# Attention row sums: four diagonal rounds of each second half move from Pool's adds to TensorE's ones matmuls

## The chip, the cores and the metric

The program runs on one core of one Trainium2 chip. The metric is the device time of one execution in microseconds (us), lowest to highest over three runs, with the median as the figure that is compared. One more execution was taken by the hardware profiler; its trace gives all durations below.

## What is computed

The program is a chain of four blocks on an input of 2 x 1024 rows of 1024, each added to its input after a layer norm. The change is in the third, causal attention with 32 heads of 32 columns. Eight groups of four heads exist:

```python
def _L1_attn_ref(x, Wq, Wkv, Wo, bo):
    ...
    q = jnp.dot(x, Wq).reshape(b, t, H, HD).transpose(0, 2, 1, 3)
    kv = jnp.dot(x, Wkv).reshape(b, t, G, 2, HD).transpose(2, 3, 0, 1, 4)
    ...
    scores = jnp.einsum('bhqd,bhkd->bhqk', q, k)
    causal = jnp.triu(jnp.ones((t, t), dtype=bool), 1)
    scores = jnp.where(causal[None, None], -jnp.inf, scores)
    weights = jax.nn.softmax(scores * (1.0 / HD ** 0.5), axis=-1)
    ctx = jnp.einsum('bhqk,bhkd->bhqd', weights, v)
    ctx = ctx.transpose(0, 2, 1, 3).reshape(b, t, d)
    return jnp.dot(ctx, Wo) + bo
```

Here b is 2, t is 1024, H is 32, HD is 32. The softmax's denominator is the sum of the exponentials over the keys of a query; the change is about how that sum is formed.

## The kernel before

The classes StageA to StageD hold the four blocks, and each engine has a hand-written order of its instructions in each. Attention is StageC (lines 1542 to 2415). Its main loop has 16 **items** `o`, one for each batch half and head group, and each item has 48 **slots** `s`: 12 **rounds** `r` of four heads `g`. A round is a key tile `kt` of 128 keys against one **half** of the queries, 512 wide. The table ROUNDS (line 1493) lists them: rounds 0 to 3 are the first half (key tiles 0 to 3, all on the diagonal, 512, 384, 256 and 128 queries wide), rounds 4 to 7 are the second half's key tiles 0 to 3 (each 512 wide, below the diagonal), and rounds 8 to 11 its key tiles 4 to 7 (diagonal: 512, 384, 256 and 128 wide).

In one slot the engines do this:

- **TensorE** (`pe`, from line 2024) computes one score tile (`pe_score`, line 1978) into one of three PSUM banks, then one tile of the row-maximum pass for a slot 60 further on (`pe_amax`, line 1960), then on some slots three matmuls of the projection for a later item (`pe_job`, lines 1936 to 1938). At the second slot of each round (`g == 1`) it multiplies the exponentials of the round two before by the values (`pe_pv`, line 1993): four matmuls of 32 output rows each, in four column groups of the array. At slot 38 there is one small transpose of the maxima (line 1966).
- **ScalarE** (`act_exp`, line 2147) writes the exponentials of a round into one of three buffers P. It waits until the round three before has been multiplied (`pv_s`) and added up (`psum_s` or `pair_s`).
- **Pool** (`pool`, from line 2369) masks the diagonal block of a diagonal round (the affine select, line 2389), and adds the round's exponentials to a running sum S in SBUF, four heads at a time (lines 2383, 2385, 2406, 2407 and 2410). VectorE makes the sum of rounds 4 and 5 (`dve_pair`, line 2244). Pool also multiplies the finished contexts by the reciprocal sums (`pool_mul`, line 2367), and for two weights computes the low parts (`POOL_W`, line 2231).
- **TensorE** then sums S over its 128 partitions by matmuls with a matrix of ones (`pe_sum`, line 2019), four matmuls of 512 columns: the first half at slot 20, the second at slot 5 of the next item. ScalarE copies that bank out (`act_evac`) at the next slots 22 and 6.
- **VectorE** reduces each tile of the maximum pass (`dve_amax`, lines 2298 and 2302), and splits projections and weights into high and low parts.

Three PSUM banks (3, 4 and 6) serve the maximum pass, the transposes and the row sums in turn. The function `tables` hands them out at build time: `turn(o, a)` takes the bank that was given back longest ago, and `keeps` is the list of banks to be taken. A bank's next user waits for the engine that read the last one (`pe_turn`).

Four items, BY_ROUND (4, 5, 14 and 15), already sum their first half another way: `pe_sums` (line 2009) multiplies each round's exponentials by the ones matrix right behind the values' product, adding in one PSUM bank over the four rounds, and Pool adds nothing there. They hold a bank from slot 9 to slot 21. Of items 14 and 15, VectorE adds the later rounds (LAST, `dve_last`).

The semaphore counts that go with Pool's adds are computed by `adds(o, r)`.

SP's queue loads and stores; among its transfers are the rows of maxima (`sp_mrow`, tile c_mT to c_Q, issued at slot 40 for the next item), without which the next item's first score cannot start.

## Time and profile before the change

| | us |
|---|---|
| median of 3 runs | 2275.1 |
| lowest, highest run | 2274.99, 2286.18 |
| profiled execution, first to last instruction (span) | 2287.7 |
| TensorE matmuls busy | 2130.1 (93%) |
| TensorE weight loads busy | 1514.9 (66%) |
| VectorE busy | 1433.9 (63%) |
| Pool busy | 998.4 (44%) |
| ScalarE busy | 919.1 (40%) |

The profiler gives no time of its own execution apart from the span, so the span stands for it; it is 0.55% above the median of the runs. Busy time is the time an engine worked, whatever else ran beside it. A matmul's end in the trace is modelled, and the next may start before it: the distance from one start to the next is what a matmul takes of TensorE. "<-" behind an idle time names what ended it.

The granted clock of TensorE was 0.964 of full speed over the span. Attention's main loop runs from about 1014 us to 1790 us of the span.

### The profile page before, as it was taken

How to read it: one execution, taken by the hardware profiler on the slowest of the kernel's cores; microseconds unless marked ns; L12 is line 12 of the kernel's file. 1: busy time of each engine (PE TensorE's matmuls, PEld its weight loads, DVE VectorE, ACT ScalarE, POOL GpSimd, SP SyncE). 2: the span in 40 equal slices, each digit the busy share in tenths (PEclk: the TensorE clock that was granted, in tenths of full speed). 3: DMA queues.
4: the chain of work that ended last, by engine and by line, in shares of the span. 5: the costliest groups of instructions: out<-in, count | busy, mean ns of one | idle time of the engine just before them, and what ended most of it. 6: DMA issues, size and time to landing. Idle time of an engine off the chain costs nothing.

```text
span 2287.7 us, 30903 instructions
## 1 busy us (share of the span) xinstructions
PE 2130.1 (93%) x10720; PEld 1514.9 (66%) x10720; DVE 1433.9 (63%) x3291; ACT 919.1 (40%) x1675; POOL 998.4 (44%) x866
## 2 busy tenths in 40 slices
PE   5889997799999999989999999899998999999998
PEld 4755555688888878855555555555554687676677
DVE  8865688677777664287665667567668555443333
ACT  5644465333333323225554455455555332221111
POOL 1343476544444430016885577667873232120000
PEclk9899998999999999989999999999987999999999
DMA  5210147222222238531224722322223475343232
GB/s 185 83 81 1 59 148 254 112 74 74 74 74 74 74 108 288 138 75 50 70 63 100 203 65 75 77 69 72 57 67 117 155 255 166 111 172 123 100 122 92
DMA packets 139594, 249.25 MB, mean 109 GB/s; under 512 B 26910, under 2 KB 69790, under 8 KB 139216
## 3 DMA queue, kind: packets, MB, share of 16 engines
q1 hardware_dynamic: 128432, 227.37, 31.3%
q10 hardware_dynamic: 11008, 19.93, 2.8%
q8 instruction: 85, 1.39, 0.3%
q14 instruction: 69, 0.57, 0.1%
HBM read 139.48 MB, written 76.02 MB: 94 GB/s over the span
## 4 chain that ended last, share of the span: by engine, by line
PE 63%; POOL 12%; DVE 8%; DMA 3%; issue 3%; SPq 2%; ACT 2%; ACTq 1%; DVEq 0%; POOLq 0%
POOL c_S L2410 7%; PE PS L2579 5%; PE PS L2583 5%; PE PS L2580 5%; PE PS L2622 5%; PE PS L1119 3%; PE PS L1118 3%; PE PS L1120 3%; PE PS L1978 3%; PE PS L1960 2%; PE PS L1993 2%; PE PS L1151 2%; PE PS L1153 2%; PE PS L1152 2%; PE PS L1936 2%
## 5 line engine op out<-in xcount | busy, mean ns | idle before, releaser
L2147 ACT ACTIVATE c_P<-PS 128x512 f32<-128x512 f32 (+3 forms) x768 | 357.6, 494 | 331.8 <-PE PS L1978 311.4
L1960 PE MATMUL PS<-c_K,c_Q 96*128 96x512 f32 (+3 forms) x768 | 278.6, 373 | 19.8 <-DVE cst L2302 14.5
L1978 PE MATMUL PS<-c_Q,c_K 97*128 97x512 f32 (+3 forms) x768 | 284.3, 384 | 12.4 <-DMA c_Q<-c_mT 9.5
L2410 POOL TENSOR_TENSOR c_S<-c_S,c_P 128x2048 f32<-128x2048 f32 (+3 forms) x94 | 272.6, 2901 | 8.5
L1978 PEld LDWEIGHTS PS<-c_Q,c_K 97*128 97x128 f32 x768 | 148.3, 195 | 181.4 <-ACT c_P L2147 97.9
L2298 DVE TENSOR_REDUCE cst<-PS 128x1 f32<-128x512 f32 x256 | 175.9, 687 | 91.6 <-PE PS L1960 91.1
L1960 PEld LDWEIGHTS PS<-c_K,c_Q 96*128 96x128 f32 x768 | 151.4, 197 | 75.9 <-DVE cst L2302 38.6
L1993 PE MATMUL PS<-c_P,c_V 128*32 128x512 f32 (+3 forms) x1536 | 170.0, 515 | 15.1 <-ACT c_P L2147 8.2
L2302 DVE CUSTOM_DVE_ANT_0 PS<-PS,maskw,cst 128x128 f32<-128x128 f32 (+3 forms) x256 | 142.8, 558 | 58.1 <-PE PS L1960 42.2
L199 POOL TENSOR_TENSOR maskw<-maskw,mhalf 128x1 f32<-128x1 f32 x64 | 36.5, 570 | 323.1 <-DVE maskw L168 323.0
L2302 DVE CUSTOM_DVE_ANT_0 PS<-PS,maskw 128x128 f32<-128x128 f32 (+3 forms) x256 | 126.4, 504 | 73.7 <-PE PS L1960 71.5
L1363 DVE SCALAR_TENSOR_TENSOR b_pr<-b_g,b_a 128x460 f32<-128x460 f32 x192 | 159.9, 869 | 1.7
L1251 ACT ACTIVATE b_g<-PS 128x460 f32<-128x460 f32 x96 | 53.1, 553 | 263.7 <-PE PS L1125 263.7
L2389 POOL TENSOR_SCALAR_AFFINE_SELECT c_P<-c_P 128x512 f32<-128x512 f32 x128 | 86.4, 675 | 163.6 <-ACT c_P L2147 163.4
L2579 PE MATMUL PS<-c_xth,d_xh 128*128 128x512 f32 x384 | 154.0, 401 | 0.0
L1461 POOL TENSOR_TENSOR b_gp<-b_g 128x230 f32<-128x230 f32 x96 | 84.8, 884 | 156.0 <-DVE b_g L1348 155.9
L1118 PE MATMUL PS<-b_w13h,b_xsh 128*128 128x460 f32 (+1 forms) x384 | 148.0, 385 | 3.9 <-DVE b_g L1348 3.9
L2580 PE MATMUL PS<-c_xtl,d_xh 128*128 128x512 f32 x384 | 149.6, 389 | 0.0
L1119 PE MATMUL PS<-b_w13l,b_xsh 128*128 128x460 f32 (+1 forms) x384 | 143.8, 374 | 0.0
L1120 PE MATMUL PS<-b_w13h,b_xsl 128*128 128x460 f32 (+1 forms) x384 | 143.1, 373 | 0.0
L1936 PE MATMUL PS<-c_xth,c_wh 128*128 128x512 f32 x304 | 126.4, 416 | 4.7 <-POOL c_wl L2231 2.3
L1937 PE MATMUL PS<-c_xtl,c_wh 128*128 128x512 f32 x304 | 122.3, 402 | 0.0
(293 smaller groups left out, 4888.3 us busy)
## 6 DMA issues: line engine op xcount, KB each, us to landing
a_xin<-in_x SPq DMA_DIRECT2D x32, 512.0 KB, 4.0
d_x<-scr SPq DMA_DIRECT2D x32, 512.0 KB, 4.4
c_Q<-c_qh SPq DMA_DIRECT2D x240, 64.0 KB, 2.0
scr<-a_xin SPq DMA_DIRECT2D x16, 512.0 KB, 5.3
b_xn<-scr SPq DMA_DIRECT2D x16, 512.0 KB, 5.7
b_x<-scr SPq DMA_DIRECT2D x16, 512.0 KB, 4.9
scr<-b_x SPq DMA_DIRECT2D x16, 512.0 KB, 2.6
scr<-b_y SPq DMA_DIRECT2D x16, 512.0 KB, 3.0
```

Source lines behind the costliest of these rows:

```text
L1118: e.matmul(o, self.xsh[:, par, i, :], wh[:, v, i, :], start=i == 0, stop=False)
L1119: e.matmul(o, self.xsh[:, par, i, :], wl[:, v, i, :], start=False, stop=False)
L1120: e.matmul(o, self.xsl[:, par, i, :], wh[:, v, i, :], start=False, stop=False)
L1960: e.matmul(bank[:, 0:hi - lo], self.Q4[0:96, 4 * (o % 3) + g, 128 * t:128 * t + 128], self.K4[0:96, HEADS[o % 8], lo:hi], start=True, stop ...
L1978: e.matmul(self.k.bank(i % 3)[:, 0:hi - lo], self.K4[0:97, HEADS[o % 8], 128 * kt:128 * kt + 128], self.Q4[0:97, 4 * (o % 3) + g, lo:hi], ...
L1993: m = e.matmul(k.bank(5)[32 * g:32 * g + 32, lo - 512 * half:512], self.V[:, kt, o // 8, HEADS[o % 8], :], P[:, g, 0:hi - lo], start=kt == ...
L2147: e.activation(self.P[:, R % 3, g, 0:hi - lo], self.k.bank(i % 3)[:, 0:hi - lo], ACT.Exp, scale=SCALE).then_inc(self.exp_s.s, 1)
L2298: e.tensor_reduce(m, r, AX, ALU.max).then_inc(self.mx_s.s, 1)
L2302: e.tensor_tensor_reduce(out=r, in0=r, in1=self.maskw[:, 512 - n:512], scale=1.0, scalar=m if lo > 0 else -3.0e38, op0=ADD, op1=ALU.max, a ...
L2410: e.tensor_tensor(S[:, :, 512 - n:512], S[:, :, 512 - n:512], P[:, :, 0:n], ADD).then_inc(self.psum_s.s, 1)
L2579: e.matmul(o, h, wh[:, c, cols], start=c == 0, stop=False)
L2580: e.matmul(o, h, wl[:, c, cols], start=False, stop=False)
```

## The change

For items 0 to 13, the second half's four diagonal rounds (ON_PE, rounds 8 to 11) are no longer added by Pool. TensorE multiplies each by the ones matrix right behind its values' product, into the bank of the second half's sum, and `pe_sum` at slot 5 of the next item adds the matmuls over S to what stands there. S then holds rounds 4 to 7: VectorE's pair and Pool's adds of rounds 6 and 7. Pool still masks rounds 8 to 11. The bank is taken at slot 41, not at slot 5 of the next item, and is given back in the order of turns at slot 5 as before. Items 14 and 15 are as they were.

```diff
--- before.py
+++ after.py
@@ -1535,6 +1535,14 @@
 
 BY_ROUND = (4, 5, 14, 15)
 
+ON_PE = (8, 9, 10, 11)
+
+
+def pool_rounds(o):
+
+    first = [] if o in BY_ROUND else [1, 1, 2, 3]
+    return first + [r for r in range(6, 12) if (o, r) not in LAST and r not in ON_PE]
+
 
 POOL_W = {(4, 8): JOB[7] + 1, (8, 9): JOB[11] + 1}
 
@@ -1633,8 +1641,10 @@
                     keeps.append(turn(A // 48, A % 48))
                 if s == 38 and o < 15:
                     keeps.append(turn(o + 1, 48))
+                if s == 4 * ON_PE[0] + 9 and o < 14:
+                    held = turn(o + 1, 50)
                 if s == 5 and o > 0:
-                    keeps.append(turn(o, 50))
+                    keeps.append(held if o < 15 else turn(o, 50))
                 if o in BY_ROUND and s == 9:
                     kept = turn(o, 49)
                 if o in BY_ROUND and s == 21:
@@ -1693,8 +1703,8 @@
     def adds(o, r, piece=1):
 
 
-        first = 10 * o - 4 * sum(b < o for b in BY_ROUND)
-        return first + (r + piece if r == 1 else r + 1 if r < 6 else r - (5 if o in BY_ROUND else 1))
+        before = sum(len(pool_rounds(b)) for b in range(o))
+        return before + 1 + pool_rounds(o).index(r) + (piece if r == 1 else 0)
 
     def dsum_s(self, n, g):
 
@@ -1994,6 +2004,8 @@
                          P[:, g, 0:hi - lo], start=kt == 0, stop=kt == 4 * half + 3, skip_group_check=True)
         if half == 0 and o in BY_ROUND:
             m = self.pe_sums(e, o, r)
+        if r in ON_PE and o < 14:
+            m = self.pe_sums(e, o, r)
         m.then_inc(self.pv_s.s, 1)
 
     @staticmethod
@@ -2003,20 +2015,23 @@
     def pe_sums(self, e, o, r):
 
         kt, lo, hi = ROUNDS[r]
-        turn = self.sum_turn(2 * o)
-        bank = self.pe_turn(e, *turn) if kt == 0 else self.turn_bank(*turn)
+        half = hi > 512
+        turn = self.sum_turn(2 * o + half)
+        first, last = (ON_PE[0], None) if half else (0, 3)
+        bank = self.pe_turn(e, *turn) if r == first else self.turn_bank(*turn)
         for g in range(4):
-            m = e.matmul(bank[32 * g:32 * g + 32, lo:512], self.k.ones[:, 0:32], self.P[:, (12 * o + r) % 3, g, 0:hi - lo],
-                         start=kt == 0, stop=kt == 3, skip_group_check=True)
+            m = e.matmul(bank[32 * g:32 * g + 32, lo - 512 * half:512], self.k.ones[:, 0:32],
+                         self.P[:, (12 * o + r) % 3, g, 0:hi - lo], start=r == first, stop=r == last, skip_group_check=True)
         return m
 
     def pe_sum(self, e, E):
 
         o = E // 2
-        e.wait_ge(*(self.dsum_s(4 if o == 14 else 10, 3) if E in (29, 31) else self.psum_s(self.adds(o, 11 if E % 2 else 3))))
-        bank = self.pe_turn(e, *self.sum_turn(E))
+        e.wait_ge(*(self.dsum_s(4 if o == 14 else 10, 3) if E in (29, 31) else self.psum_s(self.adds(o, pool_rounds(o)[-1] if E % 2 else 3))))
+        begun = E % 2 and o < 14
+        bank = self.turn_bank(*self.sum_turn(E)) if begun else self.pe_turn(e, *self.sum_turn(E))
         for g in range(4):
-            m = e.matmul(bank[32 * g:32 * g + 32, :], self.k.ones[:, 0:32], self.S[:, g, :], start=True, stop=True,
+            m = e.matmul(bank[32 * g:32 * g + 32, :], self.k.ones[:, 0:32], self.S[:, g, :], start=not begun, stop=True,
                          skip_group_check=True)
         m.then_inc(self.sum_s.s, 1)
 
@@ -2142,7 +2157,7 @@
                 e.wait_ge(*self.pair_s(4 * o3 + g + 1))
             elif (o3, r3) in LAST:
                 e.wait_ge(*self.dsum_s(LAST.index((o3, r3)), g))
-            elif r3 > 5 and o3 < 15 and g == 0:
+            elif r3 > 5 and r3 not in ON_PE and o3 < 15 and g == 0:
                 e.wait_ge(*self.psum_s(self.adds(o3, r3)))
         e.activation(self.P[:, R % 3, g, 0:hi - lo], self.k.bank(i % 3)[:, 0:hi - lo], ACT.Exp, scale=SCALE).then_inc(self.exp_s.s, 1)
 
@@ -2393,7 +2408,7 @@
                         self.low_w4(e, POOL_W[o, r], q)
                 if o > 0 and r in (0, 4):
                     self.pool_mul(e, 2 * o - (2 if r == 0 else 1))
-                if r in (0, 4, 5) or (o, r) in LAST or r < 4 and o in BY_ROUND:
+                if r not in pool_rounds(o):
                     continue
                 if lo == 128 * kt:
                     e.wait_ge(*self.diag_s(8 * o + kt + 1))
@@ -2406,7 +2421,7 @@
                         e.tensor_copy(S[:, gs, 0:128], P0[:, :, 0:128])
                         e.tensor_tensor(S[:, gs, 128:512], P0[:, :, 128:512], P[:, gs, 0:384], ADD).then_inc(self.psum_s.s, 1)
                     continue
-                e.wait_ge(*self.psum_s(self.adds(o, r - 1)))
+                e.wait_ge(*self.psum_s(self.adds(o, pool_rounds(o)[pool_rounds(o).index(r) - 1])))
                 e.tensor_tensor(S[:, :, 512 - n:512], S[:, :, 512 - n:512], P[:, :, 0:n], ADD).then_inc(self.psum_s.s, 1)
         self.pool_mul(e, 30)
```

How the instructions stand on **TensorE** at slot 41 of item 0 (the values' product of round 8; L1993 is the values' product, L1978 a score, L1960 a tile of the maximum pass, L1936 to L1938 a projection). Before:

```order
L1938 MATMUL PS<-c_xth,c_wl 128x512
L1978 MATMUL PS<-c_Q4,c_K4 128x256 [waits s_c_exp]
L1960 MATMUL PS<-c_K4,c_Q4 128x128 [waits s_c_mtc]
L1993 MATMUL PS<-c_P,c_V 32x512 [waits s_c_diag,s_c_exp]
L1993 MATMUL PS<-c_P,c_V 32x512 x3
```

With the change (the lines are 10 further on for these, and L2023 is the ones matmul of `pe_sums`):

```order
L1948 MATMUL PS<-c_xth,c_wl 128x512
L1988 MATMUL PS<-c_Q4,c_K4 128x256 [waits s_c_exp]
L1970 MATMUL PS<-c_K4,c_Q4 128x128 [waits s_c_mtc]
L2003 MATMUL PS<-c_P,c_V 32x512 [waits s_c_diag,s_c_exp]
L2003 MATMUL PS<-c_P,c_V 32x512 x3
L2023 MATMUL PS<-c_P,cst 32x512 [waits s_c_mx]
L2023 MATMUL PS<-c_P,cst 32x512 x3
```

Four ones matmuls stand behind the product, and the first waits for VectorE to have read the bank (s_c_mx).

**TensorE** at slot 5 of item 1, with the change (L2034 is `pe_sum`, over S):

```order
L2003 MATMUL PS<-c_P,c_V 32x128 x3
L2023 MATMUL PS<-c_P,cst 32x128 x4
L2034 MATMUL PS<-c_S,cst 32x512 [waits s_c_psum]
L2034 MATMUL PS<-c_S,cst 32x512 x3
L1988 MATMUL PS<-c_Q4,c_K4 128x384 [waits s_c_exp]
```

The matmuls over S stay where they were; before, their first one waited for s_c_mx also, since the bank was taken there.

**Pool** in the second half of item 0 (L2383, L2385 and L2410 are adds to S, L2389 is the mask, L2367 the product of a finished context). Before:

```order
L2383 TENSOR_TENSOR c_S<-c_S,c_P 128x1024 [waits s_c_pair,s_c_exp]
L2385 TENSOR_TENSOR c_S<-c_S,c_P 128x1024 [waits s_c_exp]
L2410 TENSOR_TENSOR c_S<-c_S,c_P 128x2048 [waits s_c_psum,s_c_exp]
L2389 AFFINE_SELECT c_P<-c_P 128x4x128 [waits s_c_exp]
L2410 TENSOR_TENSOR c_S<-c_S,c_P 128x2048 [waits s_c_psum,s_c_diag]
...
L2410 TENSOR_TENSOR c_S<-c_S,c_P 128x4x384 [waits s_c_psum,s_c_diag]
...
L2410 TENSOR_TENSOR c_S<-c_S,c_P 128x4x256 [waits s_c_psum,s_c_diag]
...
L2410 TENSOR_TENSOR c_S<-c_S,c_P 128x4x128 [waits s_c_psum,s_c_diag]
...
L2367 TENSOR_TENSOR c_cH<-c_cH,c_cS 128x512 [waits s_c_den0]
```

With the change (15 lines further on):

```order
L2398 TENSOR_TENSOR c_S<-c_S,c_P 128x1024 [waits s_c_pair,s_c_exp]
L2400 TENSOR_TENSOR c_S<-c_S,c_P 128x1024 [waits s_c_exp]
L2425 TENSOR_TENSOR c_S<-c_S,c_P 128x2048 [waits s_c_psum,s_c_exp]
L2404 AFFINE_SELECT c_P<-c_P 128x4x128 [waits s_c_exp] x5
L2382 TENSOR_TENSOR c_cH<-c_cH,c_cS 128x512 [waits s_c_den0]
```

Four adds are gone, and the masks of rounds 8 to 11 and of the next item's round 0 stand one behind the other.

## Rows read from the trace of the kernel before

**Rows 1.** The page: the span, and the engines' busy time.

```profile
span 2287.7 us, 30903 instructions
PE 2130.1 (93%) x10720; PEld 1514.9 (66%) x10720; DVE 1433.9 (63%) x3291; ACT 919.1 (40%) x1675; POOL 998.4 (44%) x866
```

**Rows 2.** Busy time by stretch (length, then PE, PEld, DVE, ACT, POOL, clock, DMA).

```profile
1014.00:1790.00 776.00, 721.04 (x4106) 428.16 (x4106) 536.93 (x1434) 417.33 (x951) 524.21 (x339) 0.96 0.31 82
```

**Rows 3.** The chain that ended last, 1014 to 1790 us, by line.

```profile
by line: POOL c_S L2410 21.8%; PE PS L1978 8.6%; PE PS L1993 6.6%; PE PS L1960 6.0%; issue 4.4%; PE PS L1936 3.9%; DVE PS L2302 3.8%; PE PS L1937 3.6%; PE PS L1938 3.6%; POOL c_P L2389 3.5%; POOL c_S L2383 3.4%; POOL c_S L2385 3.3%; DVE c_S
```

**Rows 4.** Waits, 1014 to 1790 us: total, times, longest.

```profile
ACT c_P L2147 <- POOL c_S L2410: 14.4, 19, 2.3
```

**Rows 5.** Groups by shape, 1014 to 1790 us, Pool's adds: busy, mean ns.

```profile
L2410 POOL TENSOR_TENSOR c_S<-c_S,c_P 128x2048 f32<-128x2048 f32 x28 | 128.5, 4590 | 3.1
...
L2410 POOL TENSOR_TENSOR c_S<-c_S,c_P 128x1024 f32<-128x1024 f32 x26 | 62.1, 2388 | 2.2
L2410 POOL TENSOR_TENSOR c_S<-c_S,c_P 128x1536 f32<-128x1536 f32 x14 | 48.7, 3479 | 1.1
...
L2410 POOL TENSOR_TENSOR c_S<-c_S,c_P 128x512 f32<-128x512 f32 x26 | 33.3, 1282 | 2.2
```

**Rows 6.** Timeline of PE, item 4, rounds 0 and 1: start, length.

```profile
1206.26 1.06 PE L1993 MATMUL PS<-c_P,c_V 128*32 128x512 f32 x8
1207.14 1.04 PE L2009 MATMUL PS<-c_P,cst 128*32 128x512 f32 x8
1208.11 0.39 PE L1978 MATMUL PS<-c_Q,c_K 97*128 97x256 f32 x1
...
1211.01 0.85 PE L1993 MATMUL PS<-c_P,c_V 128*32 128x384 f32 x8
1211.68 0.83 PE L2009 MATMUL PS<-c_P,cst 128*32 128x384 f32 x8
```

**Rows 7.** Timeline of PE, item 11, a product without sums.

```profile
1604.03 1.06 PE L1993 MATMUL PS<-c_P,c_V 128*32 128x512 f32 x8
1605.02 0.38 PE L1978 MATMUL PS<-c_Q,c_K 97*128 97x256 f32 x1
```

**Rows 8.** Timeline of PE, from item 11 to item 12.

```profile
1608.15 0.85 PE L1993 MATMUL PS<-c_P,c_V 128*32 128x384 f32 x8 [0.25 <-POOL c_P L2389]
...
1611.00 0.28 PE L1960 MATMUL PS<-c_K,c_Q 96*128 96x256 f32 x1
1612.31 0.64 PE L1993 MATMUL PS<-c_P,c_V 128*32 128x256 f32 x8 [1.03 <-ACT c_P L2147]
...
1616.64 0.64 PE L2019 MATMUL PS<-c_S,cst 128*32 128x512 f32 x4 [0.22 <-POOL c_S L2410]
```

**Rows 9.** Timeline of ACT, first exponentials of item 12.

```profile
1611.69 1.09 ACT L2147 ACTIVATE c_P<-PS 128x512 f32<-128x512 f32 x2 [0.59 <-POOL c_S L2410]
```

**Rows 10.** Timeline of PE, item 13, rounds 10 and 11.

```profile
1695.86 1.06 PE L1993 MATMUL PS<-c_P,c_V 128*32 128x512 f32 x8 [1.70 <-POOL c_P L2389]
...
1701.06 1.51 PE L1993 MATMUL PS<-c_P,c_V 128*32 128x384 f32 x8 [1.98 <-POOL c_P L2389]
```

**Rows 11.** Busy time by stretch, behind item 13's stall (columns as in Rows 2).

```profile
1701.00:1712.00 11.00, 10.94 (x51) 6.19 (x52) 6.21 (x16) 4.94 (x11) 10.26 (x7) 0.55 0.00 0
```

**Rows 12.** Timeline of PE, first scores of items 5 and 9.

```profile
1256.40 0.50 PE L1978 MATMUL PS<-c_Q,c_K 97*128 97x512 f32 x1 [2.23 <-DMA c_Q<-c_mT]
...
1462.52 0.79 PE L1978 MATMUL PS<-c_Q,c_K 97*128 97x512 f32 x1 [3.03 <-DMA c_Q<-c_mT]
```

**Rows 13.** Busy time by stretch, behind the first scores of items 5 and 6.

```profile
1256.00:1262.00 6.00, 5.60 (x24) 3.55 (x25) 1.54 (x7) 1.98 (x4) 1.27 (x1) 0.72 0.81 237
1309.00:1315.00 6.00, 5.99 (x21) 4.07 (x22) 1.58 (x7) 2.32 (x4) 3.58 (x3) 0.50 0.43 98
```

**Rows 14.** Timeline of DVE, slot 47 of item 11.

```profile
1610.62 0.76 DVE L2302 CUSTOM_DVE_ANT_0 PS<-PS,maskw,cst 128x512 f32<-128x512 f32 x1 [0.35 <-PE PS L1960]
```

**Rows 15.** Timeline of PE, item 5, while its first half's sum holds a bank.

```profile
1273.79 0.38 PE L1960 MATMUL PS<-c_K,c_Q 96*128 96x256 f32 x1 [0.62 <-DVE cst L2302]
```

## The prediction, made before the changed kernel was run

> **What bounds the kernel now.** I read the page first. TensorE's matmuls are busy 93% of the span, Pool's work 44% [rows 1], so over the whole kernel this change moves work from an engine with room to the fullest one. The average says nothing about the stretch where the change acts, so I asked for the main loop of attention alone: in its 776 us TensorE is busy 721.0, Pool 524.2, VectorE 536.9 [rows 2]. TensorE sits without a running matmul for 55 us there in all. The chain of waits speaks the other way: 21.8% of it, 169 us, runs over the Pool line that adds to S [rows 3], the line from which the change takes four of six adds in an item's second half. A chain names one path; where two engines run side by side, nearly equally full, shortening one gains only until the other is reached. So the waits have to be priced. ScalarE waits for Pool's adds 19 times for 14.4 us in the whole loop [rows 4], and what TensorE loses by it is read from the timeline of starts, below. The reader should see in this that Pool is back to back in the last six rounds of an item, and TensorE nearly so too.
>
> **What the change adds.** Sixteen ones matmuls for each of 14 items, in the widths 512, 384, 256 and 128. The kernel before already does such sums in four first halves, so the price stands in the trace. In item 4 the product of 512 columns starts at 1206.26, its sums at 1207.14, the next score at 1208.11 [rows 6]; that is 1.85 us for product and sums. A product without sums takes 1604.03 to 1605.02, 0.99 [rows 7]. The sums thus cost 0.86. For 384 columns the sums start 0.67 behind their product where they start 0.88 behind it at 512 [rows 6], so 128 columns are worth 0.21, and the four rounds cost 0.86 + 0.65 + 0.44 + 0.23 = 2.18 us. Nothing lies beside it, as TensorE runs its instructions in order and here one starts as the other's columns are through. For 14 items: **+30.5**. Bounds: at the bare 0.21 for each 128 columns (2.1 us) it is 29.4. If nothing were shared with the product, the sums would cost their own distance of 0.97 at 512 [rows 6], 0.11 more in each round: 36.7.
>
> What the row of the product shows is that the score after it begins late by about 0.1. The Trainium skill, TensorEngine Tiling (Array Packing), Key Properties, says that a change of tiling mode drains TensorE. The sums use the same four column groups as the product in front of them and stand directly behind it, so by that rule no further drain is paid, and the sum stays at 30.5; were each set of sums to pay for its own, it would be the 36.7.
>
> **What it removes.** Pool loses adds of 4.59, 3.48, 2.39 and 1.28 us in each of 14 items [rows 5], 11.7 us each, 164 in all. None of it is time by itself; only what waited for it counts. From item 11 to item 12 the waits are these. The product of round 9 waits 0.25 for the mask on Pool, behind the add of round 8. The product of round 10 starts 1.31 behind the tile in front of it, 1611.00 to 1612.31 [rows 8], where such a tile of 256 columns is otherwise followed after 0.2: 1.1 lost, since the exponentials wait for a buffer that Pool still adds from, until 1611.69 [rows 9]. The ones matmuls over S wait 0.22 for Pool's last add [rows 8], and by the same count of starts the first and the last of the three cost 0.4 each. Together 1.9 us. The same three stand at eight crossings (items 0 to 1, 1 to 2, 2 to 3, 6 to 7, 7 to 8, 10 to 11, 11 to 12, 12 to 13). At 9 to 10 only 0.3 is lost, at 3 to 4 nothing. With four adds gone Pool is some 10 us early there, and no piece of the wait should stay: **-15.5**.
>
> From item 13 to 14 there is no projection to fill TensorE, and Pool sets the pace: two waits of 1.70 and 1.98 [rows 10], and behind them 11 us at a granted clock of 0.55 with TensorE busy 10.9 of them [rows 11]. The waits go, 3.7. Of the slow stretch I take back 3.3 of the about 5 that the half clock costs, because VectorE's 6.2 us of work there becomes the next limit. **-7**, between -3.7 and -9.
>
> At the starts of items 5, 6 and 9 the first score waits for the row of maxima, 2.23 us, 3.03 and, at item 6, about as long as at item 5 [rows 12]. That transfer does not hang on Pool; it is issued at slot 40. But the sums of rounds 8 and 9 (0.86 + 0.65) fall between slot 40 and that score, so 1.5 us of the new work lies inside each wait, 4.5 in all. At 5 and 6 the rest of the wait is then about as short as the 1.03 of item 12, behind which no slow stretch stands, while now 6 us follow at a clock of 0.72 and at 0.50 [rows 13]. If these go it is worth 1.3 and 3 us, of which I take 3.3 together. **-7.8**, between -3 and -10.
>
> Sum of the removed: -30.3, between -22 and -35.
>
> **What it moves.** The sum's bank is now held from slot 41 to slot 5 of the next item, so the maximum pass runs on two banks for 12 slots of 14 items where it had three. A tile then waits for VectorE to have reduced the tile two before it, not three. Lay this on item 11 to 12: the tile at slot 1 starts at 1611.00 [rows 8]; the one two before, at slot 47, is being reduced from 1610.62 for 0.76 and read out behind it, until about 1611.5 [rows 14]. So 0.5 to 0.6 us is lost at that tile, and the others of the twelve fit. I take 0.55 for each of 14 items: **+7.7**. The least is 0, if the longer slots give VectorE its time. The most comes from the four first halves that already hold a bank: item 5 shows a wait of 0.62 for VectorE at one tile [rows 15] and half as much at another, 1.5 lost in the hold, 21 over 14 items. That is with VectorE splitting a weight in the same slots, which in the second half it mostly doesn't, hence the value near the low end.
>
> Two edits cost nothing. The wait for `pe_sum` is now for Pool's add of round 7, finished some 14 us earlier, so nothing is late in its stead. The release of a P buffer (`pv_s`) comes after the sums, up to 0.9 us later, but the exponentials that need it are three slots away, each of them longer than the 0.23 of a 512-column matmul.
>
> **The sum.** 30.5 + 7.7 - 30.3 = **+7.9 us**. The profiled execution would go from a span of 2287.7 [rows 1] to 2295.6. That execution lies 0.55% above the runs' median of 2275.1; the difference is carried over, and the forecast is **2283**. A measurement of this kernel can tell about 0.5% (11.4 us) from no change, so this is "the same". With the bounds of its own terms the case reaches from 2268 to 2297.
>
> **The rivals.**
>
> - *The bank hold decides* (slower). With two banks VectorE is in TensorE's way in every second half. It decides once the hold costs more than 11 us, 0.8 an item. For it: the maximum pass and VectorE are full (537 of 776 us [rows 2]), and item 5 loses 1.5 in such a hold [rows 15]. Against: the second half has fewer weight splits. Time: 2275.1 + 30.5 + 21 - 30.3 = 2296.
> - *The sums pay full price and the slow stretches stay* (slower). Sums at 36.7, the starts of 5, 6 and 9 absorb nothing beyond 1, item 13 gives back its two waits only: 36.7 + 7.7 - 15.5 - 3.7 - 1 = +24, 2299. Against it, the row of item 4 shows the sharing.
> - *Pool was the pace* (faster). If the chain is right and all of TensorE's 55 us without a matmul [rows 2] hang on Pool in the end, it is 2275.1 + 30.5 - 55 = 2251. Against it: the named waits for Pool come to a third of that.
> - *TensorE has room* (faster). Its weight loads are busy 428 of the loop's 776 us, its matmuls 721 [rows 2]. If the true load were nearer the first, sums would slip into gaps and cost nothing: 2275.1 + 7.7 - 30.3 = 2253. The Trainium skill, Perfetto Trace Analysis, Identifying the Most-Contended Engine, says that matmul busy time misleads and that the weight loads' share is the measure to use. The trace speaks against it in this case: the score behind the sums of item 4 starts 0.86 later than without them [rows 6, 7].
>
> **How the numbers follow.** Forecast 0.53, bank hold 0.17, full price 0.12, Pool the pace 0.11, room on TensorE 0.07. Faster by over 0.5% is under 2263.7: the two last rivals less a little of their own slack, 0.16. Slower is over 2286.5: the two first rivals, which reach it nearly always, and a tenth of the forecast's own spread, 0.32. The same: 0.52. The range that leaves out 2 in 10 goes from 2262 to 2300, taking in the slower rivals and leaving out the middle of the faster ones.
>
> **What would show it.** After the change, sums behind a 512-column product start 0.88 behind it and the next score 0.97 later, also in rounds 8 to 11. ScalarE's and the weight loads' waits for the line adding to S all but vanish, Pool's busy time falls by 164 us, matmul busy time in the loop rises by some 30 us. The crossings of items 6 to 7 and 11 to 12 are longer by 2.2 + 0.5 - 1.9 = 0.8 us. The waits of maximum tiles for VectorE rise by 5 to 10 us in rounds 10 and 11 and the next rounds 0 and 1; if by over 15, the bank rival is right. The first scores of items 5, 6 and 9 wait 1.5 us less. The forecast is wrong if the sums' distance behind their product is another than in item 4, if other TensorE waits go along with Pool's, or if clock stretches appear where there were none.

## The result, and the profile after

| | us |
|---|---|
| before, median of 8 runs | 2281.11 (2274.99 to 2286.18) |
| with the change, median of 8 runs | 2291.51 (2287.11 to 2293.81) |
| ratio | 1.0043, 95% interval 1.0029 to 1.0056 |
| profiled execution with the change, span | 2285.3 |

The change costs 0.43%, that is +9.8 us, between 6.6 and 12.8. (Here and below, microseconds beside a ratio are the ratio on the median of the kernel before; the two medians themselves are 10.4 apart.) The forecast was +7.9 us on 2275.1. Five more runs of the kernel before moved its median from 2275.1 to 2281.11, and so the absolute figure of 2291.5 is 8.5 above the forecast 2283, while the difference is 2 us off. The changed kernel was run again later, on another occasion and against other runs of the kernel before, with +13.2 us (below).

The page after, to be held against [rows 1]:

```profile
span 2285.3 us, 31673 instructions
PE 2141.9 (94%) x11168; PEld 1517.6 (66%) x11168; DVE 1431.9 (63%) x3291; ACT 918.1 (40%) x1675; POOL 834.1 (36%) x810
```

Pool's busy time falls by 164.3 us, which is the four adds of 14 items. The profiled span is shorter than before, although the runs are longer. The two profiled executions differ outside the loop: the loop starts 5 us earlier in this one. They also stand at opposite ends of the runs: the span of 2287.7 before is above the longest of the eight runs (2286.18), while the execution profiled here is the shortest of its eight (2287.11). So from here on only the main loop is compared, and in it first of all the places that repeat.

The main loop by stretch, against [rows 2] (length, then PE, PEld, DVE, ACT, POOL, clock, DMA):

```profile
1008.00:1784.00 776.00, 733.87 (x4542) 432.20 (x4541) 535.11 (x1430) 415.99 (x950) 357.42 (x283) 0.99 0.30 82
```

TensorE's matmuls are busy 12.8 us more of the same 776, where the prediction looked for some 30, and Pool 166.8 less. The sums' busy time is there: in the crossing from item 11 to 12 (from one first pair add to the next, see below), where the clock is at full speed in both, matmuls are busy 2.1 us more, before and after:

```profile
1589.04:1635.52 46.48, 44.15 (x261) 26.84 (x257) 33.00 (x93) 25.98 (x61) 36.43 (x23) 1.00 0.31 79
1589.03:1636.45 47.42, 46.23 (x294) 27.91 (x289) 33.00 (x95) 25.90 (x61) 24.86 (x19) 1.00 0.31 77
```

Elsewhere in the loop the granted clock was higher in this execution (0.99 against 0.96 over the whole loop), and the same matmuls are busy for a shorter time at a higher clock: a product of 384 columns is busy 1.51 us in the slow stretch of item 13 [rows 10, 11] and 0.85 at full speed [rows 8]. The prediction left that out of its 30.

The chain of waits by line, against [rows 3]:

```profile
by line: PE PS L2003 14.8%; PE PS L1988 14.8%; PE PS L1970 13.2%; PE PS L1946 7.3%; PE PS L1947 6.9%; PE PS L1948 6.9%; issue 5.6%; PE PS L2023 4.6%; DVE PS L2317 4.3%; DVE cst L2313 2.8%; DVE c_S L2259 2.1%; PE PS L2034 2.0%; DVE c_wl L224
```

Pool's add to S, 21.8% of the chain before, isn't among the lines named. Most of the chain has gone over to TensorE: values' product, scores, maximum tiles, projections, and with 4.6% the new sums (L2023). The loop did not get shorter by it. This is what a chain looks like when two engines run side by side nearly equally full: it names the one, and a relief of that one hands it to the other.

The waits for Pool's adds, against [rows 4], and of the maximum tiles for VectorE:

```profile
PEld PS L1970 <- DVE cst L2317: 40.0, 62, 2.4
PE PS L1970 <- DVE cst L2317: 15.9, 37, 1.9
...
PEld PS L2034 <- POOL c_S L2425: 11.0, 11, 2.4
...
ACT c_P L2162 <- POOL c_S L2425: 1.5, 1, 1.5
```

The same rows before, without ScalarE's, which stands in [rows 4]:

```profile
PEld PS L1960 <- DVE cst L2302: 31.5, 49, 1.9
...
PEld PS L2019 <- POOL c_S L2410: 15.3, 20, 2.4
...
PE PS L1960 <- DVE cst L2302: 11.9, 25, 1.5
```

ScalarE waited 19 times for such an add, and now waits once. The weight loads in front of the matmuls over S waited 20 times for 15.3 us and still wait 11 times for 11.0: the prediction said that these too would all but vanish, and that failed. The maximum tiles' waits for VectorE rose from 11.9 us in 25 times to 15.9 in 37 on the matmuls' row, 4.0 us in 12 more waits, and by 8.5 us on the weight loads' row. The prediction said 5 to 10, and that over 15 would speak for the bank rival.

Now the crossing from item 11 to 12, against [rows 6 to 9] (timeline of PE: start, length):

```profile
1604.03 1.07 PE L2003 MATMUL PS<-c_P,c_V 128*32 128x512 f32 x8
1604.91 1.04 PE L2023 MATMUL PS<-c_P,cst 128*32 128x512 f32 x8
1605.89 0.39 PE L1988 MATMUL PS<-c_Q,c_K 97*128 97x256 f32 x1
...
1608.70 0.85 PE L2003 MATMUL PS<-c_P,c_V 128*32 128x384 f32 x8
1609.37 0.83 PE L2023 MATMUL PS<-c_P,cst 128*32 128x384 f32 x8
...
1612.69 0.39 PE L1970 MATMUL PS<-c_K,c_Q 96*128 96x256 f32 x1 [0.33 <-DVE cst L2317]
1613.01 0.64 PE L2003 MATMUL PS<-c_P,c_V 128*32 128x256 f32 x8
1613.47 0.61 PE L2023 MATMUL PS<-c_P,cst 128*32 128x256 f32 x8
...
1617.12 0.43 PE L2003 MATMUL PS<-c_P,c_V 128*32 128x128 f32 x8
1617.36 0.40 PE L2023 MATMUL PS<-c_P,cst 128*32 128x128 f32 x8
1617.58 0.61 PE L2034 MATMUL PS<-c_S,cst 128*32 128x512 f32 x4
```

The sums start 0.88, 0.67, 0.46 and 0.24 us behind their products of 512, 384, 256 and 128 columns, and the score follows 0.98 behind the start of the widest sums. Item 4 has the same 0.88 and 0.67, and 0.97 to the score [rows 6]; its 0.46 and 0.24 are in the trace too. None of the three waits for Pool of [rows 8] is left; the product at 1613.01 follows its tile after 0.32, where it took 1.31. In their place one wait for VectorE stands, 0.33 at the tile of 256 columns. And Pool waits for ScalarE in front of its masks, 0.5 us at the second and 3 to 4 at those behind it:

```profile
1603.23 0.64 POOL L2404 TENSOR_SCALAR_AFFINE_SELECT c_P<-c_P 128x512 f32<-128x512 f32 x1 [0.51 <-ACT c_P L2162]
1607.81 0.63 POOL L2404 TENSOR_SCALAR_AFFINE_SELECT c_P<-c_P 128x512 f32<-128x512 f32 x1 [3.94 <-ACT c_P L2162]
1611.88 0.63 POOL L2404 TENSOR_SCALAR_AFFINE_SELECT c_P<-c_P 128x512 f32<-128x512 f32 x1 [3.44 <-ACT c_P L2162]
```

**A ruler for the rest.** VectorE's first pair add of an item (slot 23) has a fixed place, so the distance from one item's to the next's is the time of a crossing. Before and after, for items 11 and 12:

```profile
1589.04 0.69 DVE L2244 TENSOR_TENSOR c_S<-c_P 128x512 f32<-128x512 f32 x1
...
1635.52 0.69 DVE L2244 TENSOR_TENSOR c_S<-c_P 128x512 f32<-128x512 f32 x1
```

```profile
1589.03 0.69 DVE L2259 TENSOR_TENSOR c_S<-c_P 128x512 f32<-128x512 f32 x1
...
1636.45 0.69 DVE L2259 TENSOR_TENSOR c_S<-c_P 128x512 f32<-128x512 f32 x1
```

46.5 us before, 47.4 after: +0.9, where 2.2 + 0.5 - 1.9 = 0.8 was forecast. The two traces stand side by side at 1589.03 and part by 0.9 us in one item.

### The profile page after: what moved, and what is told of

Read it like the earlier page. It is cut to its first block, busy times and chain, and to the rows that moved or that the text cites. A ratio compares the mean times of both kernels' runs of the same rounds, so it can differ in the third digit from the quotient of the medians.

```text
span 2285.3 us, 31673 instructions
## 1 busy us (share of the span) xinstructions
PE 2141.9 (94%) x11168; PEld 1517.6 (66%) x11168; DVE 1431.9 (63%) x3291; ACT 918.1 (40%) x1675; POOL 834.1 (36%) x810
## 4 chain that ended last, share of the span: by engine, by line
PE 77%; DVE 9%; issue 4%; ACT 3%; POOL 2%; DMA 2%; SPq 1%; ACTq 1%; DVEq 0%; POOLq 0%
PE PS L2594 5%; PE PS L2003 5%; PE PS L1988 5%; PE PS L2598 5%; PE PS L2595 5%; PE PS L2637 5%; PE PS L1970 5%; PE PS L1119 3%; PE PS L1118 3%; PE PS L1120 3%; PE PS L1946 3%; PE PS L1947 3%; PE PS L1948 3%; PE PS L1151 2%; PE PS L654 2%
## 5 line engine op out<-in xcount | busy, mean ns | idle before, releaser
L1988 PE MATMUL PS<-c_Q,c_K 97*128 97x512 f32 (+3 forms) x768 | 278.4, 376 | 6.2 <-ACT c_P L2162 3.1
L1970 PEld LDWEIGHTS PS<-c_K,c_Q 96*128 96x128 f32 x768 | 148.3, 193 | 86.1 <-DVE cst L2317 47.1
L2317 DVE CUSTOM_DVE_ANT_0 PS<-PS,maskw,cst 128x128 f32<-128x128 f32 (+3 forms) x256 | 142.9, 558 | 57.6 <-PE PS L1970 41.5
L1348 DVE TENSOR_TENSOR b_g<-b_g,PS 128x460 f32<-128x460 f32 x96 | 60.4, 630 | 100.1 <-ACT b_g L1251 100.0
```

The lines of the kernel that those rows point to most:

```text
L1970: e.matmul(bank[:, 0:hi - lo], self.Q4[0:96, 4 * (o % 3) + g, 128 * t:128 * t + 128], self.K4[0:96, HEADS[o % 8], lo:hi], start=True, stop ...
L1988: e.matmul(self.k.bank(i % 3)[:, 0:hi - lo], self.K4[0:97, HEADS[o % 8], 128 * kt:128 * kt + 128], self.Q4[0:97, 4 * (o % 3) + g, lo:hi], ...
L2317: e.tensor_tensor_reduce(out=r, in0=r, in1=self.maskw[:, 512 - n:512], scale=1.0, scalar=m if lo > 0 else -3.0e38, op0=ADD, op1=ALU.max, a ...
```

## The experiments

Two theories stood against each other. That of the prediction: an item pays 2.2 us for the sums and 0.55 for the hold of the bank, and gets back what TensorE waits for Pool, 1.9 us. The rival: relieving Pool is worth a good deal more or overlaps otherwise, and the bank hold is what eats it. The first four kernels take the change apart, the next four vary one size, the last two look for a better version and repeat the changed kernel.

### One part at a time

**The hold alone.** Kernel before, with

```diff
+                if s == 41 and o < 14:
+                    held = turn(o + 1, 50)
                 if s == 5 and o > 0:
-                    keeps.append(turn(o, 50))
+                    keeps.append(held if o < 15 else turn(o, 50))
```

> The kernel before, with one edit: the bank of a second half's sum is taken at slot 41 and not at slot 5 of the next item, for items 0 to 13. No sums are moved, Pool adds as before. My theory prices the hold at 0.55 us an item where nothing else is waited for; at the eight crossings where TensorE waits 1.1 us for Pool right behind, the wait for VectorE lies inside that wait and costs nothing. So 0 to +3 us against the kernel before. The rival that the bank hold decides wants +11 us or more, up to +21.

Measured: ratio 1.0009, interval 0.999 to 1.0027 (+2 us, from -2 to +6); the crossing takes 46.5 us as before. The timeline of PE at the crossing from item 11 to 12 shows where the price went:

```profile
1607.62 0.38 PE L1962 MATMUL PS<-c_K,c_Q 96*128 96x256 f32 x1 [0.34 <-DVE cst L2304]
1608.40 0.64 PE L1995 MATMUL PS<-c_P,c_V 128*32 128x256 f32 x8 [0.41 <-ACT c_P L2149]
```

The tile waits 0.34 for VectorE, and the product right behind it waits 0.41 for ScalarE where it waited 1.03 [rows 8]. The hold's wait sits inside the wait for Pool. That the hold decides, which wanted 11 us or more, is excluded here; what the hold costs where Pool no longer covers it is measured two kernels on.

**The sums, with Pool's adds left in.** Changed kernel, with

```diff
-    return first + [r for r in range(6, 12) if (o, r) not in LAST and r not in ON_PE]
+    return first + [r for r in range(6, 12) if (o, r) not in LAST]
...
-            m = e.matmul(bank[32 * g:32 * g + 32, :], self.k.ones[:, 0:32], self.S[:, g, :], start=not begun, stop=True,
+            m = e.matmul(bank[32 * g:32 * g + 32, :], self.k.ones[:, 0:32], self.S[:, g, :], start=True, stop=True,
...
-            elif r3 > 5 and r3 not in ON_PE and o3 < 15 and g == 0:
+            elif r3 > 5 and o3 < 15 and g == 0:
```

> The changed kernel with Pool's four adds put back: Pool adds rounds 8 to 11 to S as before, the ones matmuls of these rounds run too, and the matmuls over S overwrite the bank. The output is complete. My theory: the 2.18 us of sums in an item fill the 1.9 us that TensorE waits for Pool anyway, so this is only 0 to 6 us slower than the changed kernel, +10 to +16 us against the kernel before. If instead relieving Pool is worth its 30 us by itself and does not overlap with the sums, it is +38 us.

Measured: ratio 1.006, interval 1.0041 to 1.008 (+13.7 us, from 9 to 18), as expected; a crossing takes 47.4 us. So with all of Pool's work back, the crossing is as long as with the change. The timeline of POOL shows it back to back:

```profile
1615.70 0.63 POOL L2404 TENSOR_SCALAR_AFFINE_SELECT c_P<-c_P 128x512 f32<-128x512 f32 x1
1616.42 3.47 POOL L2425 TENSOR_TENSOR c_S<-c_S,c_P 128x1536 f32<-128x1536 f32 x1
1619.84 0.63 POOL L2404 TENSOR_SCALAR_AFFINE_SELECT c_P<-c_P 128x512 f32<-128x512 f32 x1
```

and that of PE does not wait for it, only for VectorE:

```profile
1621.05 0.38 PE L1970 MATMUL PS<-c_K,c_Q 96*128 96x256 f32 x1 [0.33 <-DVE cst L2317]
1621.36 0.64 PE L2003 MATMUL PS<-c_P,c_V 128*32 128x256 f32 x8
```

The sums make TensorE late enough that Pool is no longer late. At the crossings the relief of Pool, 11.7 us an item, is worth nothing once the sums are in.

**The relief alone.** Kernel before, with rounds 8 to 11 taken out of Pool's list in items 0 to 13 and nothing in their place: no call of `pe_sums` for them, no hold.

> The kernel before without Pool's adds of rounds 8 to 11 in items 0 to 13, and without anything in their place: the denominators of the second half lack the keys 512 to 1023 (the time is that of less work). It gives what relieving Pool is worth by itself. My theory: -15.5 us at eight crossings, -4 to -9 at item 13, nothing at the first scores of items 5, 6 and 9, which wait for a transfer: -20 to -25 us. If Pool was the pace of the loop: -45 or more. If Pool's waits hide others: -10 or less.

Measured: ratio 0.9926, interval 0.9898 to 0.9953 (-17 us, from -11 to -23), where -20 to -25 was expected; a crossing takes 44.6 us, 1.9 less than before, to the tenth what the three waits came to. The loop from item 0 to item 14 is 24.1 us shorter in its profile. Of that, 8.0 us lie in the three stretches with a wait for the row of maxima (table below), where nothing was expected. PE at the crossing (items 11 to 12) runs without a wait:

```profile
1594.69 0.28 PE L1968 MATMUL PS<-c_K,c_Q 96*128 96x256 f32 x1
1594.90 0.64 PE L2001 MATMUL PS<-c_P,c_V 128*32 128x256 f32 x8
1595.47 0.50 PE L1986 MATMUL PS<-c_Q,c_K 97*128 97x512 f32 x1
```

44.6 us is thus what a crossing takes when TensorE never waits for Pool, and 46.5 what it took with Pool's adds beside it. The matmuls of the sums are then 2.2 us on top of 44.6 and the hold 0.6: 47.4.

**The relief with the hold.** As above, and the bank taken at slot 41.

> As the kernel without Pool's adds of rounds 8 to 11 and nothing in their place (denominators of the second half incomplete), and in addition the bank is held from slot 41 to slot 5 of the next item. Against that kernel it gives the price of the hold where Pool no longer covers it. My theory: +7.7 us above it (0.55 us an item), so -12 to -17 us against the kernel before; the rival that the hold decides wants +15 to +21 us above it.

Measured: ratio 0.9937, interval 0.9916 to 0.9959 (-14.4 us, from -9 to -19). Against the kernel without the hold that is some 2.5 us more, where 7.7 was expected, and the two intervals overlap, so the runs don't settle the size. The crossings do, for one crossing: 45.2 us, 0.6 above 44.6, with the same wait of 0.3 in the timeline:

```profile
1596.40 0.38 PE L1970 MATMUL PS<-c_K,c_Q 96*128 96x256 f32 x1 [0.32 <-DVE cst L2315]
```

Behind item 3 the hold costs nothing (51.3 us with it and without). So 0.6 holds for the crossings, and a sum of 7.7 over 14 items is not shown.

### One size changed

**The sums twice.** The changed kernel, with a second set of the four ones matmuls behind the first in rounds 8 to 11:

```diff
+        if half:
+            for g in range(4):
+                m = e.matmul(bank[32 * g:32 * g + 32, lo - 512 * half:512], self.k.ones[:, 0:32],
+                             self.P[:, (12 * o + r) % 3, g, 0:hi - lo], start=False, stop=False, skip_group_check=True)
```

> The changed kernel with each set of ones matmuls of rounds 8 to 11 issued twice (these keys count double in the denominators). It gives the price of the sums where Pool is already relieved. My theory: each further set costs its columns, 0.86 + 0.65 + 0.44 + 0.23 = 2.2 us an item, +31 us for 14 items over the changed kernel less some 4 us inside the waits for the row of maxima, so +35 to +41 us against the kernel before; a crossing of items takes 49.6 us, where the changed kernel takes 47.4. If TensorE had room the period would stay near 47.4.

Measured: ratio 1.0171, interval 1.0146 to 1.0196 (+39 us, from 33 to 45); a crossing takes 49.6 us. The timeline of PE has the price of one set as the distance of the two:

```profile
1681.37 1.06 PE L2003 MATMUL PS<-c_P,c_V 128*32 128x512 f32 x8
1682.25 1.04 PE L2023 MATMUL PS<-c_P,cst 128*32 128x512 f32 x8
1683.11 1.04 PE L2027 MATMUL PS<-c_P,cst 128*32 128x512 f32 x8
```

0.86 us at 512 columns. A second set makes a crossing 2.2 us longer, the whole of its price. That excludes the rival that TensorE has room.

**Round 8 alone.** ON_PE is `(8,)`, everything else follows from it.

> Of the four rounds only round 8 goes to TensorE (one set of 512 columns, the widest add of Pool's), Pool keeps rounds 9 to 11. My theory: relief of one add of 4.59 us already ends all three waits for Pool at a crossing (1.9 us), for 0.86 us of sums and 0.6 us of hold: 46.5 - 1.9 + 0.86 + 0.6 = 46.1 us a crossing, and 4 to 8 us faster than the kernel before over all. If the whole relief of 11.7 us were needed, the crossing would take more than 46.5 us and the time be 0 to 10 us above.

Measured: 2275.31 us against 2282.35, ratio 0.9966, interval 0.9951 to 0.9982 (-7.8 us, from -4 to -11); a crossing takes 46.1 us, as worked out. This is 0.34% faster than the kernel before, small but clear of noise, and the changed kernel is slower than the kernel before.

**Round 9 alone.** ON_PE is `(9,)`.

> Only round 9 goes to TensorE (384 columns), Pool keeps rounds 8, 10 and 11; the bank is held from slot 45. The wait of 0.4 us for the mask behind the add of round 8 stays, the other two (1.5 us) go, for 0.65 us of sums and 0.6 us of hold: 46.5 - 1.5 + 0.65 + 0.6 = 46.2 us a crossing, 0 to 6 us faster than the kernel before over all.

Measured: ratio 0.9977, interval 0.9962 to 0.9992 (-5.2 us, from -2 to -9); a crossing takes 46.2 us, as worked out. Its interval overlaps that of round 8 alone, so the runs don't rank the two.

**The whole change in items 5, 8 and 13.**

> The whole change, but for items 5, 8 and 13 only, where the two traces show the stretch that follows shortened by 2.2, 3.1 and 3.7 us (for items 5 and 8 the first score behind waits for a transfer, for 13 Pool is the pace). If these gains belong to the items: 6 to 9 us faster than the kernel before. If they are the scatter of that transfer and of the clock from one execution to the next, only item 13's is left: 0 to 4 us faster.

Measured: ratio 0.9988, interval 0.9973 to 1.0004 (-2.7 us, from -6 to +1). The profile of this kernel has the stretches behind items 5, 8 and 13 at 48.7, 63.8 and 47.1 us, where before they were 51.2, 65.4 and 50.5. The gain of 6 to 9 us that two traces seemed to promise isn't there. The interval speaks for the second reading, that the transfer and the clock scatter from one execution to the next, without excluding all of the first.

### A better version, and the change again

**Round 8 alone, but not in items 3 and 9.**

> Round 8 alone goes to TensorE, in all of items 0 to 13 but 3 and 9, the two behind which TensorE does not wait for Pool. With these two in, the traces show the stretches behind them longer by 0.8 and 1.2 us than before. My theory: those 2.0 us come back, so 0.5 to 3 us less than with all 14 items and 8 to 11 us faster than the kernel before. If the places where Pool is waited for don't matter and the gain is spread over all items, it loses a seventh of the gain: 6 to 7 us faster.

Measured: 2272.43 us against 2279.99, ratio 0.9976, interval 0.9963 to 0.9989 (-5.5 us, from -2.5 to -8; the medians are 7.6 apart). The 8 to 11 us that were expected are missed, and no gain over all 14 items shows. The two stretches did go back, to 51.3 and 47.5 us as before. But the loop in its profile, 685.4 us from item 0 to 14, is no shorter than with all 14 items, 684.6, since other stretches scatter by more. The two versions can't be told apart.

**The changed kernel again.**

> The changed kernel again, on the same chip as the other runs. It stands here so that the changed kernel and the variants are compared against the same runs of the kernel before: +8 to +12 us, and again 47.4 us a crossing.

Measured: 2292.45 us against 2279.99, ratio 1.0058, interval 1.0045 to 1.0071 (+13.2 us). The crossings take 47.4 us again. The time is a little above the 8 to 12 us expected.

### The stretches side by side

Time from one item's first pair add to the next's, from the timeline of VectorE of each kernel, in us. "Crossing" is the value shared by items 1 to 2, 6 to 7, 10 to 11, 11 to 12 and 12 to 13.

| kernel | crossing | 3 to 4 | 4 to 5 | 5 to 6 | 8 to 9 | 9 to 10 | 13 to 14 | 0 to 14 |
|---|---|---|---|---|---|---|---|---|
| before | 46.5 | 51.3 | 59.2 | 51.2 | 65.4 | 47.5 | 50.5 | 698.8 |
| hold alone | 46.5 | 51.3 | 59.7 | 47.5 | 65.0 | 47.8 | 50.9 | 695.8 |
| sums and adds | 47.4 | 53.4 | 58.4 | 49.3 | 61.7 | 51.4 | 49.6 | 704.7 |
| relief alone | 44.6 | 51.3 | 56.8 | 47.0 | 64.0 | 47.2 | 48.8 | 674.7 |
| relief and hold | 45.2 | 51.3 | 57.8 | 46.8 | 63.5 | 47.8 | 45.7 | 676.7 |
| the change | 47.4 | 53.5 | 58.4 | 49.0 | 62.3 | 51.3 | 46.8 | 702.3 |
| the change again | 47.4 | 53.4 | 60.0 | 51.2 | 65.1 | 50.0 | 47.5 | 709.7 |
| sums twice | 49.6 | 55.6 | 60.6 | 51.2 | 61.8 | 53.5 | 50.3 | 731.1 |
| round 8 | 46.1 | 52.1 | 57.1 | 47.5 | 61.7 | 48.7 | 47.2 | 684.6 |
| round 9 | 46.2 | 51.9 | 57.6 | 47.5 | 60.1 | 47.2 | 52.7 | 688.2 |
| items 5, 8 and 13 | 46.5 | 51.3 | 59.9 | 48.7 | 63.8 | 47.5 | 47.1 | 691.8 |
| round 8, not 3 and 9 | 46.1 | 51.3 | 58.7 | 50.4 | 61.6 | 47.5 | 45.4 | 685.4 |

The crossing column repeats to a tenth or two within an execution, and for the changed kernel from one execution to the next (the two kernels without adds have single crossings of 45.6 and 45.4 beside their others). The columns 4 to 5, 5 to 6 and 8 to 9 do not: one and the same kernel has 49.0 and 51.2 at 5 to 6, and 62.3 and 65.1 at 8 to 9. The last column carries that scatter. It is why the profile of the change shows the loop only 3.5 us longer and the second profile of the same kernel 10.9, on either side of the +9.8 of the runs.

## Why the prediction was right

- **The sums, +30.5.** Right. The distances of item 4 came back in all four widths, and a second set costs 0.86 at 512 columns and 2.2 us at a crossing (49.6 against 47.4). The prediction had two prices for an item, 2.2 us as in item 4 and 2.6 if nothing were shared with the product; 2.2 is what was measured. By the rule that it draws on (the Trainium skill, TensorEngine Tiling (Array Packing), Key Properties), a change of tiling mode drains TensorE, and sets in one mode would pay nothing more; the traces agree: a set behind a like set starts after 0.86 us at 512 columns, four times the 0.21 of 128.
- **The waits for Pool, -1.9 at a crossing.** Right in size (44.6 against 46.5), but put down to the relief of Pool. The kernel with sums and adds shows that the sums alone take these waits in; the relief then adds nothing at a crossing. The step's number holds, its reason is one of two that overlap, and the sum may count it once only, as it did.
- **Item 13, -7.** The size came near, the way to it was wrong in part. The stretch went from 50.5 to 46.8 and 47.5 with 2.2 of sums and 0.6 of hold in it, so 5.8 to 6.5 us went. The prediction took both waits of [rows 10] away. Only the second, 1.98 us, is gone. The first stands in every kernel, for its mask is behind Pool's add of round 7, which stays on Pool. With the change:

```profile
1692.37 4.56 POOL L2425 TENSOR_TENSOR c_S<-c_S,c_P 128x2048 f32<-128x2048 f32 x1
1696.89 1.21 POOL L2404 TENSOR_SCALAR_AFFINE_SELECT c_P<-c_P 128x512 f32<-128x512 f32 x2
```

```profile
1697.66 1.06 PE L2003 MATMUL PS<-c_P,c_V 128*32 128x512 f32 x8 [1.71 <-POOL c_P L2404]
```

  So the waits gave 2.0 us and not 3.7, and the rest, 3.8 to 4.5 us where 3.3 was forecast, goes along with the granted clock: 0.79 over the stretch before, 0.95 and 0.96 in the two executions with the change. That the relief of Pool brings the clock back isn't shown. The kernel with the relief alone has no second wait either, and its stretch is at 0.81 and takes 48.8 us:

```profile
1682.04:1732.56 50.52, 43.59 (x232) 23.41 (x225) 35.62 (x99) 26.79 (x66) 28.44 (x17) 0.79 0.22 62
1683.84:1730.66 46.82, 40.94 (x264) 20.84 (x257) 35.59 (x99) 26.71 (x66) 16.78 (x13) 0.95 0.23 67
1663.05:1711.83 48.78, 43.21 (x232) 23.05 (x225) 35.30 (x101) 26.31 (x64) 16.77 (x13) 0.81 0.22 62
```

  (Before, with the change, relief alone.) With sums and adds the second wait is 0.82 us and the stretch takes 49.6. That the two errors partly cancel is luck.
- **The transfers behind items 4, 5 and 8, -7.8.** The direction is right, the size is scatter and the cause stays open. The waits for the row of maxima were 2.23, 2.30 and 3.03 us. In the changed kernel only the last is left:

```profile
1460.93 0.50 PE L1988 MATMUL PS<-c_Q,c_K 97*128 97x512 f32 x1 [2.24 <-DMA c_Q<-c_mT]
```

  In its second execution they were 0.33, none and 1.87. That is 5.3 and 5.4 us less in all, where 4.5 was forecast, and with the sums twice 0.42 us is left of all three, so sums do fit into these waits. But the waits shrink without any sums too: with the relief alone they were 1.27, none and 2.88, with relief and hold only 2.53 at the last was left. The three stretches took 6.1 us less than before in the first execution of the change, 0.5 more in the second, and 8.0 less with the relief alone, all against one execution of the kernel before. How much the sums save there can't be read from that.
- **The bank hold, +7.7.** Right in place, and right in size at a crossing: 0.6 us, at the tile of slot 1. Behind item 3 it cost nothing, and neither the runs (2.5 us) nor the loop (2.0) with the relief show 7.7 in all. That it costs nothing as long as Pool is waited for was not in the prediction, and made no difference to the sum, in which those waits are gone.
- **Two places that the crossings hide.** Behind items 3 and 9, where TensorE hardly waited for Pool, nothing pays for the sums: +2.2 and +2.5 to +3.8 us. That was in the sum.
- **The range.** The bounds of the terms don't add up to the case of 2268 to 2297 that the prediction names. Added, they give 29.4 + 0 - 35 = -5.6 at the low end and 36.7 + 21 - 22 = +35.7 at the high one, that is 2270 to 2311.
- **The rivals.** Bank hold, room on TensorE and Pool as the pace are each excluded by a run. Full price is excluded by the distances.

The sum came to +7.9, the runs to +9.8 and +13.2 with intervals from 6.6 to 16.2. Outside the three stretches with the transfer, the loop is 9.6 us longer in the first execution of the change and 10.4 in the second, where the forecast's terms give 7.5 (2.73 for each of 11 items, less 15.5 and 7). So the part that repeats was forecast to within 3 us. That the second set of runs lies above the forecast is not explained part by part. In that execution's profile, the stretch from item 0 to 1 alone has 48.9 us, 1.5 more than the other crossings (below), and the three stretches with the transfer took 6.6 us more than in the first. Whether such things lie in the kernel or in the occasion stays open.

## What to carry to other kernels

Where two engines run side by side nearly equally full, price a shift between them by the starts on the fuller one: what each moved instruction adds from start to start, against the waits that it fills. The share of the chain (21.8% here, 169 us) overstated the relief: with 164 us of adds left out altogether the loop gave back 24 us and the runs 17. And move only as much as ends the waits: one of four adds ended them all (46.1 us a crossing), the other three were paid for without return (47.4).

## What the runs showed of the hardware

- **A wait can be filled instead of removed.** Ones matmuls on the waiting engine made Pool's adds of 11.7 us an item free at the crossings (47.4 us with them and without), with no change to Pool at all. This was not expected to be complete.
- **Column groups stay cheap behind one another.** Four fp32 matmuls of 32 output rows in four column groups cost 0.21 us for each 128 columns, whether behind the values' product or behind a like set. At 512 columns a set starts 0.88 us behind its product (item 4, the change, the doubled kernel) and 0.86 behind a like set (the doubled kernel).
- **The same wait is followed by a fall of the clock in one execution and not in the next.** In the second execution of the changed kernel, the stretch from item 0 to 1 is 1.5 us longer than the other crossings:

```profile
1029.50:1078.40 48.90, 48.10 (x295) 28.79 (x298) 33.22 (x93) 26.29 (x61) 24.88 (x19) 0.96 0.14 35
```

  A fall to half clock (0.50, 1.2 GHz) reaches into its start, and in front of the fall TensorE waited 2.00 us for Pool:

```profile
1024.64 1.06 PE L2034 MATMUL PS<-c_S,cst 128*32 128x512 f32 x8 [2.00 <-POOL c_S L2425]
```

```profile
1023.00:1026.00 3.00, 1.36 (x10) 0.45 (x10) 0.79 (x3) 0.36 (x1) 1.50 (x2) 1.00 0.00 0
1026.00:1029.00 3.00, 3.00 (x15) 1.98 (x14) 1.54 (x4) 2.52 (x5) 0.00 (x0) 0.57 0.01 3
1029.00:1032.00 3.00, 3.00 (x13) 0.87 (x11) 2.96 (x9) 1.33 (x3) 0.00 (x0) 0.50 0.03 3
```

  In the first execution the same matmul waited 1.99 us, and the clock stayed at 1.00:

```profile
1024.15 1.06 PE L2034 MATMUL PS<-c_S,cst 128*32 128x512 f32 x8 [1.99 <-POOL c_S L2425]
```

```profile
1025.00:1028.00 3.00, 3.00 (x26) 1.87 (x26) 1.66 (x4) 2.32 (x5) 0.00 (x0) 1.00 0.00 1
```

  Item 13 shows the same: behind its first wait of 1.7 us, which every kernel has, the clock over the stretch is anything from 0.76 (round 9 alone) to 0.96 (round 8, not 3 and 9). What decides it is open. The prediction named a clock stretch at a new place as a sign of being wrong; the one above is new, but came in one execution of two. A gain of the clock that stands in one trace is therefore no sure term of a sum.
